# Moving side work to other places inside the turns of the last attention stage

## The chip, the cores and the metric

The kernel runs on one core of one Trainium2 chip. The metric is the device time of one execution in microseconds (us). A profiled execution gives the trace, whose times run from the start of its span.

## What is computed

The reference is a decoder of two layers over 32 sequences of 128 tokens with 256 features, all in float32. Each layer adds three blocks to a running x: layer 0 a state-space block, a cross attention and an attention with a mixture of experts; layer 1 a recurrence, an attention and a mixture of experts. The change lies in the last two blocks, here cut short:

```python
# layer 1, attention: 16 heads of 16 features, over x and over the context, mixed by a gate
q, k, v = split(x @ Wqkv + bqkv);  qa, ka, va = split(ctx @ Wqkv_aux + bqkv_aux)
h_main = softmax(q @ k.T * scale) @ v
h_aux  = softmax(q @ ka.T * scale) @ va
x = x + (h_main * (1 - gate) + h_aux * gate) @ Wo + bo
# layer 1, experts: 2 of 8 per token
xf = layernorm(x)
scores = sigmoid(xf @ gate_w.T + balance_bias)
w, idx = top_k(scores, 2);  w = w / (w.sum(-1) + 1e-6)
x = x + sum over the two chosen experts of w * (silu(xf @ w1[e].T) @ w2[e].T)
```

## The kernel before

The 32 sequences are 8 groups of 4 (512 tokens, `NG = 8`). The attention in question has the tag "e"; its tiles begin with `e_`. It takes one **turn** per group, and a turn has 8 **pairs** of units; a unit is 8 maps of 128x128. For each unit TensorE (PE) makes the scores (line 1390), VectorE (DVE) takes the maximum (1447) and subtracts it (1451), ScalarE (ACT) takes the exponential (1511), GpSimd (POOL) adds halves and quarters of the rows (1544, 1547), PE transposes the maps (1399) and ACT copies them (1507). For each pair DVE finishes the sums and inverts them (1458, 1462, 1465: "invert"), PE turns the inverses (1421), ACT copies them (1517, tile `e_rT`), PE multiplies by the values (1413), and DVE scales and joins the result (1478, 1480: "mix").

Beside these pairs a turn carries **side work** for other groups:

- front: twelve products for the next group, through the one PSUM bank `FB` (two transposes of the normalised x, then q, k, v), each copied away by ACT (lines 1286, 1290, 1297, 1305);
- early: statistics (DVE 1223), scale (POOL 1240 to 1243) and normalisation (ACT 1271) for the group after that;
- back: the two output products of the group before (PE 1574, `FB` too) and the additions into X (DVE 1605, 1607);
- routing of the group before: statistics (DVE 765), scale (POOL 781 to 784), normalised rows (ACT 792), two transposes (PE 806) and copies (ACT 798), the product with the gate weights (PE 812), the addition of the bias (DVE 774), an exponential (ACT 828), the choice of two experts (DVE 836 to 866) with a ranking product (PE 820 to 823), and eight indirect DMAs from POOL that write the rows to their expert's place in DRAM (878, "scatters").

In the last turn there is no next group. Instead the turn holds the first output product of its own group, a total (PE 885) and the **early table**: 21 chained small DVE operations plus the first (926 to 943) that work out for the first 21 places of the expert list where each starts and which expert it belongs to. Each of the chain waits for the one before. `ready_places` is raised between line 908 and line 941.

The order of all this is written by hand. The pairs' program of each engine is a generator that stops at certain places; the side work carries due places, and `weave` (line 34) runs a side step at the first stop whose number is not below its due place:

```python
def weave(main, side):
    due = next(side, None)
    for step in main:
        while due is not None and due <= step:
            due = next(side, None)
```

In pair d (0 to 7) PE stops at 10d (after the next pair's scores, ahead of the transposes of unit 2d+1), 10d+2 (ahead of the values), 10d+5 (ahead of the turning of the inverses and the transposes of unit 2d+2) and 10d+8. DVE stops at 10d+2 (after the softening of unit 2d+2, ahead of invert), 10d+4 (ahead of the softening of unit 2d+3), 10d+6 (ahead of mix) and 10d+8. ACT stops at 10d+2 (ahead of the exponential of unit 2d+2), 10d+4 (ahead of the copy of the inverses and of the maps of unit 2d+2), 10d+6 (ahead of the exponential of unit 2d+3) and 10d+8. POOL stops at 10d (ahead of the sums of unit 2d+2), 10d+4 (ahead of those of unit 2d+3) and 10d+8. So a due place of 17 and one of 18 are the same place on PE; 12 and 13 are not.

All engines run their own queue in order, and a step whose input is not there holds back all behind it. `FB` is one bank: its users follow one another in an order (`fb_order`) that is worked out from the same due places.

After the last turn the stage goes over to the expert list (`list_experts`, lines 2626 to 2780): SyncE (SP) waits for the scatters of group 6 and for `ready_places`, then loads rows and weights place by place (2677, 2680), PE multiplies (2705, 2718), POOL adds the results to the output by indirect DMAs (2778). The routing of the last group (`LAST["route"]`) is woven into this list.

## Time and profile before

| what | value |
|---|---|
| median of 3 runs (lowest, highest) | 3130.05 us (3126.87, 3141.59) |
| the profiled execution's own time | 3133.9 us |
| its span | 3131.8 us |
| busy, share of the span: PE, DVE, ACT, POOL | 86%, 61%, 49%, 48% |
| first and last maximum (line 1447) of this attention | 2214.5, 2821.2 us |
| first load of the expert list | 2832.69 us |
| last scatter of the kernel begins | 3123.1 us |

The attention "e" is thus about 620 of the 3132 us, and the expert list about 290. The three runs lie 14.7 us apart. The spans of the trace are hardware records of each instruction; PE's are modelled at their ends, POOL's are rough.

### The profile page before, as it was taken

How to read it: one execution, taken by the hardware profiler on the slowest of the kernel's cores; microseconds unless marked ns; L12 is line 12 of the kernel's file. 1: busy time of each engine (PE TensorE's matmuls, PEld its weight loads, DVE VectorE, ACT ScalarE, POOL GpSimd, SP SyncE). 2: the span in 40 equal slices, each digit the busy share in tenths (PEclk: the TensorE clock that was granted, in tenths of full speed). 3: DMA queues.
4: the chain of work that ended last, by engine and by line, in shares of the span. 5: the costliest groups of instructions: out<-in, count | busy, mean ns of one | idle time of the engine just before them, and what ended most of it. 6: DMA issues, size and time to landing. Idle time of an engine off the chain costs nothing.

```text
span 3131.8 us, 49455 instructions
## 1 busy us (share of the span) xinstructions
PE 2695.4 (86%) x16576; PEld 1837.2 (59%) x16576; DVE 1900.0 (61%) x3513; ACT 1523.1 (49%) x2641; POOL 1499.7 (48%) x1619
## 2 busy tenths in 40 slices
PE   5888888876988888879999999899888888878997
PEld 2333333323666566645788887697455555557886
DVE  3788888784888788863222222501688988883211
ACT  4566665553777666630122221443666666643322
POOL 3577666673555577625322222200345555553443
PEclk8999999988999999989999999899999999978998
DMA  9700000001005000002377775200000100006875
GB/s 324 245 0 1 0 1 1 1 0 37 15 20 190 1 1 0 1 22 95 117 212 209 209 212 146 71 1 1 1 18 30 37 33 31 22 20 188 228 216 167
DMA packets 137955, 244.73 MB, mean 78 GB/s; under 512 B 15936, under 2 KB 111424, under 8 KB 127040
## 3 DMA queue, kind: packets, MB, share of 16 engines
q1 hardware_dynamic: 111168, 207.61, 20.1%
q0 software_dynamic: 26592, 34.63, 5.6%
q8 instruction: 109, 1.79, 0.2%
q14 instruction: 86, 0.70, 0.1%
HBM read 151.28 MB, written 92.73 MB: 78 GB/s over the span
## 4 chain that ended last, share of the span: by engine, by line
PE 35%; DVE 6%; issue 6%; POOL 5%; ACT 2%; DMA 1%; another core or an unknown queue 0%; POOLq 0%; DVEq 0%; ACTq 0%
PE PS L2442 11%; PE PS L2398 6%; PE PS L2066 4%; PE PS L2705 3%; PE PS L2718 3%; POOL e_hs L1544 2%; DMA out<-e_dead,f_token 1%; DVE e_mx L1447 1%; POOL e_qs L1547 1%; PE PS L1399 1%; POOL rows_in_place L878 1%; PE PS L2057 1%; PE PS L1337 1%; DVE e_pr L1451 1%; DVE e_den L1458 1%
## 5 line engine op out<-in xcount | busy, mean ns | idle before, releaser
L578 POOL TENSOR_TENSOR u_in<-dtx,b_rep 128x512 f32<-128x512 f32 x256 | 325.4, 1294 | 201.3 <-ACT b_rep L559 200.1
L594 DVE TENSOR_TENSOR_SCAN state<-PS,u_in 128x512 f32<-128x512 f32 x256 | 312.3, 1220 | 59.3 <-POOL u_in L578 34.9
L551 PE MATMUL PS<-scaled,ident 128*128 128x512 f32 x512 | 295.6, 661 | 28.7 <-DVE scaled L588 28.7
L2459 ACT ACTIVATE d_act_b<-PS 128x256 f32<-128x256 f32 (+2 forms) x192 | 76.5, 400 | 446.4 <-PE PS L2442 426.4
L1544 POOL TENSOR_TENSOR e_hs<-e_pr 128x512 f32<-128x512 f32 x128 | 163.0, 1273 | 236.5 <-ACT e_pr L1511 232.9
L1544 POOL TENSOR_TENSOR u_hs<-u_pr 128x512 f32<-128x512 f32 x128 | 166.3, 1299 | 215.1 <-ACT u_pr L1511 214.6
L2442 PE MATMUL PS<-d_unit_T,d_w 128*128 128x256 f32 (+1 forms) x1280 | 260.6, 356 | 1.1 <-ACT d_unit_T L2452 1.1
L2362 POOL DMA_INDIRECT out_by_token<-d_y_rows,d_token x71 | 110.8, 1561 | 300.2 <-DVE d_y_rows L2489 201.6
L2468 DVE TENSOR_TENSOR d_hid<-d_act_b,PS 128x256 f32<-128x256 f32 (+2 forms) x192 | 84.4, 441 | 279.9 <-ACT d_act_b L2459 245.6
L567 ACT ACTIVATE PS<-dt,decay_rate 128x508 f32<-128x508 f32 x256 | 173.4, 686 | 138.0 <-DVE state L594 136.2
L2442 PEld LDWEIGHTS PS<-d_unit_T,d_w 128*128 128x128 f32 x1280 | 221.0, 190 | 26.3 <-DVE d_hid L2468 1.3
L588 DVE TENSOR_TENSOR scaled<-state,PS 128x512 f32<-128x512 f32 x256 | 169.4, 664 | 55.9 <-PE PS L532 44.3
L1447 DVE TENSOR_REDUCE u_mx<-PS 128x8 f32<-128x1024 f32 x128 | 155.9, 1218 | 67.9 <-PE PS L1390 67.8
L2398 PE MATMUL PS<-d_w,d_hid 128*128 128x256 f32 x824 | 186.8, 380 | 3.6 <-DVE d_hid L2468 2.6
L2778 POOL DMA_INDIRECT out<-e_dead,f_token x71 | 110.8, 1561 | 158.1 <-DVE f_token L2756 68.2
L1507 ACT ACTIVATE e_pT<-PS 128x1024 f32<-128x1024 f32 x128 | 130.8, 1022 | 103.2 <-PE PS L1399 103.2
L1447 DVE TENSOR_REDUCE e_mx<-PS 128x8 f32<-128x1024 f32 x128 | 155.8, 1217 | 40.6 <-PE PS L1390 40.5
L2398 PEld LDWEIGHTS PS<-d_w,d_hid 128*128 128x128 f32 x824 | 155.6, 190 | 30.2 <-issue 7.5
L1399 PE MATMUL PS<-ident,e_pr 128*128 128x128 f32 x1024 | 148.2, 292 | 25.8 <-ACT e_pr L1511 25.3
L1507 ACT ACTIVATE u_pT<-PS 128x1024 f32<-128x1024 f32 x128 | 131.2, 1025 | 74.2 <-PE PS L1399 73.9
L551 PEld LDWEIGHTS PS<-scaled,ident 128*128 128x128 f32 x512 | 97.2, 204 | 117.9 <-DVE scaled L588 87.1
L1451 DVE TENSOR_TENSOR u_pr<-PS,u_mx 128x1024 f32<-128x1024 f32 x128 | 156.7, 1224 | 9.3 <-POOL u_hs L1544 2.2
(453 smaller groups left out, 6145.2 us busy)
## 6 DMA issues: line engine op xcount, KB each, us to landing
d_w<-in_d_w SPq DMA_DIRECT2D x42, 1024.0 KB, 5.8
e_dead<-in_f_w SPq DMA_DIRECT2D x40, 1024.0 KB
rows_in_place<-blank SPq DMA_DIRECT2D x136, 272.0 KB, 4.1
d_w<-in_d_w SPq DMA_DIRECT2D x42, 512.0 KB
rows_by_expert<-zeros SPq DMA_DIRECT2D x36, 272.0 KB, 3.1
d_unit_rows<-rows_by_expert SPq DMA_DIRECT2D x31, 272.0 KB
e_dead<-rows_in_place SPq DMA_DIRECT2D x31, 272.0 KB
X<-in_x SPq DMA_DIRECT2D x8, 512.0 KB, 11.2
```

The costliest lines, as they stand in the source:

```text
L551: nc.tensor.matmul(YB[:, c], ident[:], scaled[:, (KD * n + c) % RC], start=False, stop=n == NS - 1).then_inc(m_y, 1)
L567: nc.scalar.activation(seqs(DECAY[:, k % RD])[:, :, 1:L], seqs(dt[:, p, c])[:, :, 1:L], ACT.Exp, scale=decay_rate[:, c * NS + n:c * NS + n ...
L578: nc.gpsimd.tensor_tensor(u_in[:, k % RU], dtx[:, p, c], b_rep[:, n % RB], ALU.mult).then_inc(m_u, 1)
L588: nc.vector.tensor_tensor(scaled[:, k % RC], state[:, k % 2], CB, ALU.mult).then_inc(m_hc, 1)
L594: nc.vector.tensor_tensor_scan(state[:, k % 2], DECAY[:, k % RD], u_in[:, k % RU], 0.0, ALU.mult, ALU.add).then_inc(m_h, 1)
L1399: step = nc.tensor.transpose(TR[:, m], pr[:, i % 2, m], ident[:])
L1447: nc.vector.tensor_reduce(mx[:, i % 2], scores_of(i), AX.X, ALU.max).then_inc(maxed, 1)
L1451: nc.vector.tensor_tensor(pr[:, i % 2], scores_of(i), mx[:, i % 2].unsqueeze(2).broadcast_to([128, MAPS, L]), ALU.subtract).then_inc(shift ...
L1507: nc.scalar.activation(pT[:, i % 2].rearrange("p h q -> p (h q)"), flat(PS[:, 4:6]), ACT.Copy).then_inc(taken, 1)
L1544: nc.gpsimd.tensor_tensor(hs[:, i % 2], pr[:, i % 2, :, 0:L // 2], pr[:, i % 2, :, L // 2:L], ALU.add).then_inc(halved, 1)
L2398: step = nc.tensor.matmul(out_h[:, n], hid[:, p, f, row:row + 128], w_down[:, r, f], start=f == 0, stop=f == FC - 1)
L2442: step = nc.tensor.matmul(b, wt[:, r, c, f * 128:f * 128 + 128], x, start=c == 0, stop=c == KD - 1)
```

## The change

Only numbers in the tables of due places are changed (`PLAN["e"]`, `ROUTE`, `LAST`). No operation is added or removed, and the sequence of the users of `FB` stays the same. The routing of the last group, `LAST["route"]`, and the due places of the total stay.

```diff
-        "e": dict(front=[2, 12, 18, 18, 22, 42, 48, 52, 55, 60, 62, 70],
-                  taken=[2, 14, 14, 18, 22, 42, 46, 52, 54, 58, 64, 74], back=[0, 8], out_at=[2, 8],
-                  early=[16, 30, 48]),
+        "e": dict(front=[2, 13, 17, 17, 22, 41, 48, 51, 55, 59, 62, 71],
+                  taken=[1, 14, 15, 17, 23, 44, 45, 51, 53, 58, 63, 76], back=[0, 4], out_at=[2, 8],
+                  early=[16, 23, 47]),
     }
-    ROUTE = dict(stats=14, scale=8, norm=18, turn=[25, 32, 32], taken=[26, 28], add=36, exp=34,
-                 route=[36, 46, 46, 48], rank=50, scatter=[50, 50, 54, 58, 58, 64, 68, 68])
-
-    LAST = dict(back=[52, 0], out_at=[54, 2], total=54, early_table=58, late_total=58, late_table=62,
+    ROUTE = dict(stats=13, scale=8, norm=18, turn=[28, 30, 32], taken=[28, 28], add=34, exp=31,
+                 route=[36, 46, 46, 48], rank=49, scatter=[49, 49, 49, 52, 64, 77, 77, 77])
+
+    LAST = dict(back=[50, 0], out_at=[49, 2], total=54, early_table=71, late_total=58, late_table=62,
```

Put through the stops above, these steps really move (all others fall on the same stop as before):

| step | engine | stop before | stop after |
|---|---|---|---|
| front 1, second transpose | PE | 12 | 15 |
| front 11, last value product | PE | 70 | 72 |
| copy of q, first half (front 2) | ACT | 14 | 16 |
| copy of k (front 4) | ACT | 22 | 24 |
| copy of q, second half (front 5) | ACT | 42 | 44 |
| last copy of values (front 11) | ACT | 74 | 76 |
| second output product of the group before | PE | 8 | 5 |
| scale for the group after next | POOL | 30 | 24 |
| transposes of the routed rows | PE | 25, 32 | 28, 30 |
| first copy of them | ACT | 26 | 28 |
| bias added to the router's sums | DVE | 36 | 34 |
| exponential of them | ACT | 34 | 32 |
| eight scatters | POOL | 50, 50, 54, 58, 58, 64, 68, 68 | 50, 50, 50, 54, 64, 78, 78, 78 |
| last turn: first output product of its group | PE | 52 | 50 |
| last turn: its addition into X | DVE | 54 | 52 |
| last turn: early table, three parts | DVE | 58, 62, 62 | 72, 74, 76 |

## Rows read from the trace of the kernel before

**Rows 1.** Busy time by window, one line a turn; the columns stand on top
```profile
core 0: us, PE busy (x) PEld busy (x) DVE busy (x) ACT busy (x) POOL busy (x), PEclk, DMA share, GB/s
...
2525.66:2600.79 75.13, 64.12 (x579) 42.97 (x579) 67.45 (x130) 49.59 (x72) 43.65 (x49) 0.98 0.09 30
...
2754.66:2831.98 77.32, 51.77 (x443) 37.39 (x442) 61.23 (x128) 33.15 (x41) 36.14 (x38) 0.72 0.06 22
```

**Rows 2.** Waits of DVE, 2525.66 to 2600.79: us in total, times, longest
```profile
DVE e_mx L1447 <- PE PS L1390: 2.6, 5, 0.7
...
DVE e_den L1458 <- POOL e_qs L1547: 1.6, 2, 1.1
...
DVE e_part L1478 <- ACT e_rT L1517: 0.4, 1, 0.4
```

**Rows 3.** Timeline, a turn's start: start, us, engine, line, operation [idle <-releaser]
```profile
2523.89 0.38 ACT L1517 ACTIVATE e_rT<-PS 128x256 f32<-128x256 f32 x1 [0.25 <-PE PS L1421]
...
2524.62 1.89 PE L1574 MATMUL PS<-e_wo,e_oT 128*128 128x256 f32 x8
...
2526.91 1.27 POOL L1544 TENSOR_TENSOR e_hs<-e_pr 128x512 f32<-128x512 f32 x1 [1.11 <-ACT e_pr L1511]
...
2527.28 1.45 DVE L1607 TENSOR_TENSOR X<-X,e_o 128x512 f32<-128x512 f32 x1
...
L1607 DVE TENSOR_TENSOR X<-X,e_o x16: 691/886/1457, 2293.5 to 2840.8; 128x512 f32<-128x512 f32 x16
```

**Rows 4.** Timeline of the same turn, pairs 1 to 3
```profile
2535.51 0.69 ACT L1290 ACTIVATE e_q<-PS,e_bq 128x512 f32<-128x512 f32 x1 [2.82 <-PE PS L1337]
...
2550.70 0.69 DVE L1458 TENSOR_REDUCE e_den<-e_qs 128x16 f32<-128x512 f32 x1 [1.07 <-POOL e_qs L1547]
...
2550.77 1.95 PE L812 MATMUL PS<-f_wr,f_xT 128*128 128x8 f32 x16 [0.69 <-ACT f_xT L798]
...
2550.91 1.07 POOL L1241 TENSOR_TENSOR e_rs<-e_rs,neg_half 128x4 f32<-128x4 f32 x1
...
2551.71 0.36 DVE L1465 COPY e_rec<-e_den 128x128 f32<-128x128 f32 x2
...
2554.38 0.18 DVE L774 TENSOR_TENSOR f_lg<-PS,f_v 128x32 f32<-128x32 f32 x1
```

**Rows 5.** Timeline, its pair 5, then pairs 0 and 5 of the last turn
```profile
2573.49 1.26 POOL L1544 TENSOR_TENSOR e_hs<-e_pr 128x512 f32<-128x512 f32 x1 [0.46 <-issue]
...
2756.87 0.69 DVE L1605 TENSOR_TENSOR e_o<-PS,e_bo 128x512 f32<-128x512 f32 x1 [1.47 <-PE PS L1574]
...
2801.58 2.63 PE L1574 MATMUL PS<-e_wo,e_oT 128*128 128x256 f32 x8
```

**Rows 6.** Timeline of the last turn's end: DVE, PE, POOL and SP's queue
```profile
2809.97 0.16 DVE L926 TENSOR_TENSOR f_count<-PS,f_first_row 128x8 f32<-128x8 f32 x1
...
2814.30 0.16 DVE L934 TENSOR_TENSOR_SCAN f_ends<-f_ones,f_units_e 128x8 f32<-128x8 f32 x1
...
2819.09 0.17 DVE L943 TENSOR_TENSOR f_sent<-f_sent,f_units_e 128x8 f32<-128x8 f32 x1
...
2821.37 0.69 PE L1421 MATMUL PS<-ident,e_rec 128*128 128x128 f32 x2 [6.13 <-DVE e_rec L1465]
...
2827.95 0.69 DVE L1458 TENSOR_REDUCE e_den<-e_qs 128x16 f32<-128x512 f32 x1 [3.58 <-POOL e_qs L1547]
...
2829.36 0.96 POOL L878 DMA_INDIRECT rows_in_place<-f_rows,f_slot  x1 [0.30 <-issue]
...
2831.98 0.42 DVE L1478 TENSOR_TENSOR e_part<-PS,e_rT 128x256 f32<-128x256 f32 x1 [2.66 <-ACT e_rT L1517]
...
2832.69 0.40 SPq L2677 DMA_DIRECT2D e_dead<-rows_in_place  x1
```

**Rows 7.** What SP's queue waited for, 2700 to 2900 us
```profile
SPq L2669 <- DMA rows_in_place<-f_rows,f_slot: 72.7, 1, 72.7
```

**Rows 8.** Busy time by window, the expert list, columns as in group 1
```profile
2900.00:3000.00 100.00, 100.00 (x491) 88.07 (x490) 20.90 (x78) 30.03 (x83) 47.63 (x32) 1.00 0.83 228
```

## The prediction

> **What bounds the kernel now.** I read the busy time by window first. The change touches only the turns of the attention "e", so its turns are the place to look. A turn in the middle takes 75.13 us, and DVE is busy for 67.45 us of it; PE has 64.12, ACT 49.59, POOL 43.65 [rows 1]. DVE bounds these turns. Then the waits of DVE: within that turn it waits 2.6 us for scores (five times), 1.6 us for the sums of POOL (twice) and 0.4 us for the copied inverses, 4.6 us in all [rows 2]; what is left of the 7.7 us are gaps between instructions. So moving side work can't give more than about 4.6 us a turn plus what DVE's own instructions are stretched by. It can cost more, because a step that DVE reaches too early makes it wait with everything behind it.
>
> The last turn is another case: 77.32 us, DVE busy 61.23 [rows 1], so it waits far more, and the timeline shows for what. The early table stands between two softenings and the next invert, from 2814.30 to 2819.26, and PE's turning of the inverses stands idle for 6.13 us behind it. At the end of the turn DVE waits 3.58 us for POOL and 2.66 us for ACT with nothing to do [rows 6]. Then SP's queue loads the first rows of the expert list, at 2832.69; it had waited for a scatter to land [rows 7], whose issue ended at 2830.32 [rows 6], so landing took 2.37 us. In the list PE is busy for 100.00 of 100 us [rows 8]: the list takes its time wherever it starts, and a start that is x us earlier ends the kernel x us earlier.
>
> **The change part by part, in a middle turn.** No instruction is added or removed, so the sum consists of shifts in waits. Steps whose due place changes within the same stop cost nothing.
>
> (a) The second output product (PE 1574, 1.89 us) goes from behind the turning of the inverses and the transposes of unit 2 to ahead of them. What follows on PE's queue comes 1.9 us later: ACT's copy of the inverses, which ended at 2524.27 [rows 3], ends near 2526.1. DVE's mix, with which the turn's window begins, wants it at 2525.66 [rows 1], so it waits 0.4 us. Unit 3's exponential is late by as much, and so POOL's sum from 2526.91 to 2528.18. This takes it off DVE's addition into X: that took 1.45 us from 2527.28, ending 0.55 us after POOL's, while the shortest of its 16 instances took 0.69 [rows 3]. So 0.76 us come back, and half of it goes in the later sums. Between +0.4 and -0.8 us; I take 0, as gain and loss come from the same shift.
>
> (b) ACT's copy of q stood ahead of the inverses and of the maps and let ACT wait 2.82 us for its product [rows 4]. It goes behind them. DVE did not wait there (its waits on the copied inverses are 0.4 us in the turn [rows 2]), so nothing is won at once; the second transpose goes behind the values, the products of q and k come some 0.6 us later, and with them the next scores. 0 to +0.3 us; I take 0.2.
>
> (c) Pairs 2 and 3: the exponential of unit 7 no longer stands behind the copy of the routed rows, which would shorten DVE's wait of 1.07 us for the sums [rows 4]. But POOL's scale chain, 1.07 us for its power [rows 4] and three shorter steps, now stands right ahead of those sums. The transposes go behind PE's own, and the scores of unit 8 come about 0.6 us later, into the same wait. Between -0.9 and +0.6; I take 0.
>
> (d) The bias addition (DVE 774) ran at 2554.38, behind the softening of unit 9. It now stands directly behind the invert, which ends at 2552.07, and needs PE's product, which ends at 2552.72 [rows 4]. DVE waits 0.65 us there, with the softening of unit 9 queued behind it. ACT's exponential of the router also moves, ahead of the exponential of unit 8, and waits for the same addition, so unit 8's exponential, PE's transposes and ACT's copy of them come later too. They have room as long as DVE is the bound. The ends are 0, if the product comes earlier with unit 7's exponential (c), and +1.95, if the product's whole length passes through ACT and PE to the next scores. I take 0.35, near the middle between 0 and the 0.65 that the rows show, for the product should come a little earlier.
>
> (e) Three scatters ahead of the sums of unit 12 instead of two: these came at 2573.49 [rows 5], and one scatter is 0.96 us and a gap of 0.30 [rows 6], 1.3 us. At most +1.0 us on POOL, which waits for ACT elsewhere; on DVE 0 to +0.5, I take 0. The three at the end of the turn stand ahead of the next turn's sums of unit 2, and POOL waits for ACT there too: 0, or in the worst case the same +0.5. The last value product and its copy move by one stop behind work of the pair itself: 0.
>
> Sum per middle turn: 0 + 0.2 + 0 + 0.35 + 0 = about +0.5 us; six turns (those of groups 1 to 6; the first carries no routing) give +3 us. With all ends: -1.7 to +3.8 us a turn.
>
> **In the last turn.** The second output product of group 6 comes earlier, and here DVE waited 1.47 us for it [rows 5]: -1.4 us. It is followed by a stretch with (c) and (d) as above: about +0.1. The group's own first product, 2.63 us on PE at 2801.58 [rows 5], now goes ahead of the transposes of unit 11, which come at least as much later. DVE has that product's addition into X to do meanwhile, which also comes earlier; I count +0.3 us for it in the next step, and at most 2.6.
>
> The early table: its second and third part hold DVE for 4.96 us, and the first, from 2809.97 [rows 6], is mostly beside the scores of the next pair, which DVE would else wait for. All this leaves the place ahead of invert: 5 to 6 us, of which I let 4.8 reach the last invert, as ACT and PE of the pair then bind (with the 0.3 above). The last invert, which ended at 2829.32 (2831.98 less 2.66), would end at 2824.5. The first part fits into DVE's wait of 3.58 us ahead of it. Parts two and three follow: `ready_places` after 4.4 us, at 2828.9; mix at 2829.5 instead of 2831.98. On POOL three scatters instead of two follow the last sums: the last one would begin at 2829.36 - 4.8 + 1.3 = 2825.9 and land at 2829.2. SP goes at the later of 2828.9 and 2829.2: 3.5 us earlier than 2832.69. Together with the 1.3 us from the turn's start: -4.8 us. The ends: -7 (only the table's block counts, and the early product adds all it can) and 0 (the list starts no earlier because the scatters that were put back gate it).
>
> **Sum.** 3133.9 + 3.0 - 4.8 = 3132.1 us against the profiled execution. That lies 3.85 us above the median of the three runs, so the median would be 3128.2; I say 3128.
>
> **A rule against (a) and (c).** The row of the addition into X, 1.45 us beside POOL's sum and 0.69 alone, shows that the two engines hold one another up [rows 3]. The Trainium skill, page "SBUF — State Buffer", section "Summary: rules for kernel authors", says that a DVE instruction with two inputs in SBUF and a GpSimd instruction that reads SBUF block each other for their whole length, and advises to schedule whichever is off the critical path; by it, every side step moved next to such a pair may cost a whole POOL instruction. What would follow from rows alone: one more of DVE's two-input steps a turn that falls under a sum is +0.76 us, seven turns +5 us, so 3133; one fewer gives 3123. It lies within the range.
>
> **The rivals.**
>
> 1. The turns get better, not worse: ACT's waits of 2.82 us and PE's late turning go, and with them most of DVE's wait of 1.07 us and the stretch of 0.76 us. For it: each is in the rows [rows 3, 4]. Against it: the chain of POOL is put just there. At -1.8 us a turn, 6 x -1.8 - 4.8 = -15.6: 3114.5. Chance 0.15.
>
> 2. Slower: DVE and ACT reach the bias addition too early (d). It waits for the product with the gate weights, and the exponential of unit 8 waits behind it on ACT; if PE and ACT can't take that in, each turn pays 1.95 us, and with the other ends of (b) and (e) up to 3.2. Seven turns: +14 to +22, less 4.8 for the end: 3139 to 3147 against the median. It decides from the point where the product ends over 1.5 us behind the invert (0.65 now). For it: the gate product follows two transposes that are themselves moved back. Against it: 1.07 us of waiting right before can absorb it. Chance 0.10, a third of it beyond +0.5%.
>
> 3. The end gives nothing: the scatters moved to the last stop, or the table, gate the list just as late, and turns go as forecast: 3130 + 3 - 1.4 = 3131.6. Against it: both came out at 2829 above, with 3.5 us to spare. Chance 0.15.
>
> The forecast itself has 0.60. A measurement of this kernel can tell about 0.5% (15.7 us) from no change; the three runs alone spread over 14.7 us. Rival 1 passes that bound in a good half of its cases, plus a little from runs that spread: faster 0.13; slower 0.06; within 0.5% 0.81. The range, 3113 to 3142, holds rival 1 at its size, the forecast, rival 3 and the lower end of rival 2.
>
> **What would show it.** (a) In a middle turn the copy of the inverses of pair 0 ends about 1.9 us later against the turn, and the second addition into X takes near 0.7 us. (c) DVE's wait for the sums in pair 3 is below 1.07 us. (d) DVE waits for line 812 ahead of line 774, by 0.65 us or so. The length of a middle turn is then 75.6 us, give or take one. In the last turn no wait of 6 us is left on the turned inverses, the table stands behind the last invert, and from the turn's first mix (2754.66 here) to SP's first load there are 73.2 us instead of 78.0. The list itself keeps its length. I am wrong if middle turns change by over 2 us, or if the distance from that mix to SP's load does not shrink.

## The result, and the profile after

| | kernel before | changed kernel |
|---|---|---|
| median (lowest, highest), 6 runs each | 3130.59 (3126.87, 3141.59) | 3112.86 (3110.43, 3123.00) |
| the profiled execution's own time, span | 3133.9, 3131.8 | 3123.0, 3121.1 |
| ratio, 95% interval | | 0.9942 [0.9929, 0.9956] |

The change saves 17.7 us, 0.6%. The forecast was 3128, so a gain of 2; the time fell just below the range (3113). The sign was right and the size far off.

In the trace I measure the stage from its first mix to SP's first load of the expert list, since what lies outside differs between executions of the same code. Before: from 2228.28 to 2832.69 us, 604.4. After: from 2219.83 to 2805.70 us, 585.9. That is 18.5 us less, of the size of what the medians differ by. Outside, the changed kernel's profiled execution (the slowest of its six) reached the stage 8.4 us earlier and spent 16.3 us more from that load to its end (before: 299.1, after: 315.4). A second profiled execution of it spent 303.4 us there, and those of all experiments 299 to 306, so it does not come with the edit. PE is as full as in [rows 8] from 2900 to 3000 us; in the last 75 us of that execution it waits 9.8 us in all for weights of the experts to land, where the kernel before has 1.9 and the second execution 3.0.

Busy time by window of the changed kernel, one middle turn and then the last turn; columns as in [rows 1]:

```profile
2513.77:2588.43 74.66, 62.60 (x581) 42.06 (x580) 68.14 (x129) 49.84 (x71) 43.16 (x49) 1.00 0.09 30
2739.08:2805.48 66.40, 45.09 (x438) 31.93 (x436) 58.89 (x127) 33.04 (x41) 35.94 (x39) 0.81 0.07 26
```

The last turn (from its first to its last mix) is 10.9 us shorter; with SP's load, which now follows that last mix by 0.22 us instead of 0.71, it is 11.4. The middle turn is only 0.5 us shorter. What is left comes from turns 1 and 6, which no row of mine had looked at:

| us | turn 0 | 1 | 2 | 3 | 4 | 5 | 6 | last, to SP's load | stage |
|---|---|---|---|---|---|---|---|---|---|
| before | 69.54 | 77.19 | 75.53 | 75.12 | 75.13 | 75.60 | 78.27 | 78.03 | 604.4 |
| after | 69.95 | 74.66 | 74.66 | 74.67 | 74.66 | 76.10 | 74.55 | 66.62 | 585.9 |
| difference | +0.41 | -2.53 | -0.87 | -0.45 | -0.47 | +0.50 | -3.72 | -11.41 | -18.5 |

**The turn's start, after** (timeline, answers to [rows 3]; columns: start, us, engine, line, operation):

```profile
2511.05 1.99 PE L1574 MATMUL PS<-e_wo,e_oT 128*128 128x256 f32 x8
...
2513.30 0.38 ACT L1517 ACTIVATE e_rT<-PS 128x256 f32<-128x256 f32 x1 [1.79 <-PE PS L1421]
...
2513.77 0.42 DVE L1478 TENSOR_TENSOR e_part<-PS,e_rT 128x256 f32<-128x256 f32 x1 [0.15 <-ACT e_rT L1517]
...
2515.16 0.69 DVE L1607 TENSOR_TENSOR X<-X,e_o 128x512 f32<-128x512 f32 x1
...
2516.21 1.27 POOL L1544 TENSOR_TENSOR e_hs<-e_pr 128x512 f32<-128x512 f32 x1 [1.96 <-ACT e_pr L1511]
L1607 DVE TENSOR_TENSOR X<-X,e_o x16: 691/693/694, 2285.2 to 2813.0; 128x512 f32<-128x512 f32 x16
```

The copy of the inverses ends 0.09 us ahead of the mix that wants it, where there were 1.39. POOL's half sums begin 2.44 us behind the mix instead of 1.25, and all sixteen additions into X take 0.69 us, none 1.45. This is step (a) as foretold, though the copy comes 1.3 us later against the mix and not 1.9, and the mix waits 0.15 us for it instead of the 0.4 foretold.

**The invert of pair 3, after** (answers to [rows 4]), and behind it two rows of the kernel before that [rows 4] does not have:

```profile
2536.30 1.93 PE L812 MATMUL PS<-f_wr,f_xT 128*128 128x8 f32 x16
...
2537.09 0.69 DVE L1458 TENSOR_REDUCE e_den<-e_qs 128x16 f32<-128x512 f32 x1 [0.41 <-POOL e_qs L1547]
...
2538.38 0.19 DVE L774 TENSOR_TENSOR f_lg<-PS,f_v 128x32 f32<-128x32 f32 x1
...
2538.60 0.23 ACT L828 ACTIVATE f_lg<-f_lg 128x32 f32<-128x32 f32 x1 [1.07 <-DVE f_lg L774]
```

```profile
2553.97 1.92 PE L1399 MATMUL PS<-ident,e_pr 128*128 128x128 f32 x8
...
2554.59 0.23 ACT L828 ACTIVATE f_lg<-f_lg 128x32 f32<-128x32 f32 x1 [2.01 <-DVE f_lg L774]
```

The wait for the sums is 0.41 us instead of 1.07, as (c) said. But DVE does not wait for the gate product, against (d): it ends at 2538.23, ahead of invert (2538.46). ACT waits 1.07 us for the addition; in the kernel before it had waited 2.01.

**The end of the last turn, after** (answers to [rows 6]; then SP's wait, to [rows 7]):

```profile
2796.96 0.16 DVE L926 TENSOR_TENSOR f_count<-PS,f_first_row 128x8 f32<-128x8 f32 x1
...
2799.71 0.69 DVE L1458 TENSOR_REDUCE e_den<-e_qs 128x16 f32<-128x512 f32 x1 [0.85 <-POOL e_qs L1547]
...
2801.00 0.17 DVE L934 TENSOR_TENSOR_SCAN f_ends<-f_ones,f_units_e 128x8 f32<-128x8 f32 x1
...
2802.33 1.01 POOL L878 DMA_INDIRECT rows_in_place<-f_rows,f_slot  x1 [0.30 <-issue]
...
2805.28 0.17 DVE L943 TENSOR_TENSOR f_sent<-f_sent,f_units_e 128x8 f32<-128x8 f32 x1
2805.48 0.42 DVE L1478 TENSOR_TENSOR e_part<-PS,e_rT 128x256 f32<-128x256 f32 x1
2805.70 0.40 SPq L2677 DMA_DIRECT2D e_dead<-rows_in_place  x1
SPq L2669 <- DMA rows_in_place<-f_rows,f_slot: 63.2, 1, 63.2
```

The wait of 6.13 us on the turned inverses is gone. The first part of the table lies in DVE's wait for POOL, of which 0.85 us are left out of 3.58; parts two and three run behind the last invert, while PE and ACT turn and copy its inverses. The last scatter lands 2.36 us after its issue ends (2803.34 to 2805.70), and SP starts by it. The order of these events is the one that the prediction had given.

### The profile page after: what moved, and what is told of

The parts are those of the page before. It is cut to its first block, busy times and chain, and to the rows that moved or that the text cites. A ratio compares the mean times of both kernels' runs of the same rounds, so it can differ in the third digit from the quotient of the medians.

```text
span 3121.1 us, 49454 instructions
## 1 busy us (share of the span) xinstructions
PE 2683.0 (86%) x16576; PEld 1830.6 (59%) x16576; DVE 1899.2 (61%) x3513; ACT 1524.5 (49%) x2641; POOL 1494.5 (48%) x1619
## 4 chain that ended last, share of the span: by engine, by line
PE 33%; POOL 8%; issue 6%; DVE 6%; DMA 2%; ACT 2%; POOLq 0%; SPq 0%; DVEq 0%; ACTq 0%
PE PS L2442 11%; PE PS L2398 6%; PE PS L2066 4%; POOL e_hs L1544 3%; PE PS L2705 3%; PE PS L2718 3%; POOL e_qs L1547 2%; DMA out<-e_dead,f_token 2%; POOL rows_in_place L878 1%; PE PS L2057 1%; DVE e_mx L1447 1%; DVE e_pr L1451 1%; PE PS L2427 0%; PE PS L1337 0%; PE PS L2215 0%
## 5 line engine op out<-in xcount | busy, mean ns | idle before, releaser
L1399 PE MATMUL PS<-ident,e_pr 128*128 128x128 f32 x1024 | 139.4, 280 | 28.6 <-ACT e_pr L1511 28.3
```

The lines of the kernel that those rows point to most:

```text
L1399: step = nc.tensor.transpose(TR[:, m], pr[:, i % 2, m], ident[:])
```

## The experiments

Turns below are read as in the table above: from first mix to first mix. The window of pair d runs from the mix of pair d to the next mix, so it holds the invert of pair d+1. Stage, turns and pairs of a run come from its one profiled execution. Two of the changed kernel gave 585.9 and 586.0 us; single turns with the same instructions differ by up to 2 us between executions, as experiments 2 and 3 show.

**1. The table alone.** `early_table=58` becomes 71.

> Only the early table goes to due place 71; all else is the kernel before. Theory 1 (what the profile after shows: the whole table block of 6.9 us was on DVE's path, and nothing of it comes back behind the last invert): from the last turn's first mix to SP's first load there are 78.0 - 7 = 71 us, SP's load is set by the scatter that lands last, and the whole kernel is 7 us faster (ratio 0.9978). Theory 2 (my prediction: the scores and the late transposes cover part of it): 4.8 us or less, 73.2 to 74.5 us. Middle turns keep 75.1 us under both.

Ratio 0.9986 [0.9968, 1.0004]. The last turn to SP's load takes 72.14 us instead of 78.03; its pair 5 falls from 14.31 to 7.47 and its pair 6 grows from 8.36 to 10.87. Stage 598.5. One us of these 5.9 lies in the first five pairs, above all in pair 0 (11.72 to 10.75), ahead of all that moved. From the sixth mix to SP's load it is 23.4 against 18.5 us. So the table by itself gives some 4.9 us, not the 3.5 of my sum nor the 7 of theory 1.

**2. The whole line of the last turn** (`LAST` as changed, and the router's `rank=49`, which keeps the order of `FB`).

> The table and the last group's own first product with its addition move (the whole LAST line of the change; the rank product's due place goes from 50 to 49, which is the same stop). Theory 1: the product adds at most 0.5 us to what the table alone gives, so 71 to 71.5 us from first mix to SP's load. Theory 2 (the product ahead of the transposes keeps PE busy and its clock at full level, and helps): about 69 us.

Ratio 0.9984 [0.9972, 0.9997]; last turn 72.31, stage 599.0. The group's earlier output product adds nothing to the table. Turns 5 and 6, where nothing was moved, are worth a look: 77.20 and 76.60 us, where the kernel before has 75.60 and 78.27. The one with the granted clock at 0.86 in pair 0 is turn 5 here and turn 6 there. So with the same instructions such a fall costs 1.6 us, in either turn.

**3. The routing alone** (`ROUTE` as changed, all else as before).

> Only the ROUTE line moves. My prediction: a middle turn gets 0.35 to 0.6 us longer (75.5 to 75.7), since DVE waits ahead of the bias addition. Rival: the turn gets shorter, since the copies of the routed rows no longer stand ahead of the attention's own: 74.5 or less. In the last turn the three scatters behind the last sums make SP's load 1.3 us later than before by the prediction, unless pairs 2 to 4 give back as much: 78 to 79 us against 75 to 76 by the rival.

Ratio 0.9977 [0.9962, 0.9992], stage 598.0, turns 76.65, 74.22, 74.23, 76.97, 75.34, 75.34, last turn 75.66. Two turns are as the rival said (74.5 or less), the others fit neither. The last turn is 2.4 us shorter: its first four pairs give 4.5 (pair 3 falls from 12.99 to 11.49, pair 0 from 11.72 to 9.92), the rest of the turn takes 2.1 back.

What separates turn 2 (74.22) from turn 2 of experiment 6 (74.98), which has the same instructions and the full clock too, is pair 0: 11.84 us against 12.60. The addition into X and POOL's half sums begin within 0.04 us of each other here, and which of them is long depends on which comes second. Turn 2, then turn 4:

```profile
2376.23 0.69 DVE L1607 TENSOR_TENSOR X<-X,e_o 128x512 f32<-128x512 f32 x1
2376.24 1.81 POOL L1544 TENSOR_TENSOR e_hs<-e_pr 128x512 f32<-128x512 f32 x1 [0.99 <-ACT e_pr L1511]
...
2524.64 1.27 POOL L1544 TENSOR_TENSOR e_hs<-e_pr 128x512 f32<-128x512 f32 x1 [0.94 <-ACT e_pr L1511]
2524.68 1.77 DVE L1607 TENSOR_TENSOR X<-X,e_o 128x512 f32<-128x512 f32 x1
```

**4. The plan alone** (`PLAN["e"]` as changed, all else as before).

> Only the PLAN line of e moves. My prediction: a middle turn stays within 0.2 us of 75.13, and the last turn is 1.4 us shorter (76.6 us from first mix to SP's load), as DVE no longer waits 1.47 us for the second output product. Rival: the q copy that no longer blocks ACT, and the product ahead, give the whole gain of a middle turn, 74.7 us or less.

Slower: ratio 1.0040 [1.0019, 1.0061], stage 614.2, turns 76.70, 78.25, 78.41, 78.41, 78.40, 79.24. A third of the change, taken alone, costs 9.8 us of stage, although the last turn is 3.2 us shorter (74.87); both theories are missed. The windows of pairs 0, 1 and 2 of turn 3 (columns as in [rows 1]; the third number from the end is the granted clock) say what is odd:

```profile
2452.90:2464.69 11.79, 8.91 (x71) 5.95 (x70) 11.37 (x30) 6.91 (x9) 5.59 (x8) 0.86 0.14 46
2464.69:2474.46 9.77, 7.98 (x69) 4.41 (x68) 6.70 (x13) 7.57 (x12) 4.55 (x6) 1.00 0.00 0
2474.46:2485.59 11.13, 8.97 (x86) 7.15 (x87) 8.59 (x19) 5.70 (x9) 5.03 (x7) 0.85 0.01 2
```

TensorE's granted clock falls in pair 0 and again in pair 2, in each of turns 2 to 5, and the pair that follows the first fall is 9.77 us where the kernel before has 7.55.

**5. Does the clock do it? The plan alone, and a little work that nobody reads.** Four transposes of the identity go into the free bank `FB`, in every turn but the last, 28 in all, after the same wait as the next product:

```diff
+                if table and j == 1 and g > 0:
+                    yield 12
+                    after(pe, empty, product("front", g, j))
+                    for k in range(GS):
+                        nc.tensor.transpose(FB[:, k * L:k * L + L], ident[:], ident[:])
                 yield at[j]
```

> The old kernel with the new PLAN line (turns of 78.4 us, with the granted clock at 0.86 in pair 0 of turns 2 to 5) and, ahead of the values of pair 1, four more PE transposes (0.66 us) of the identity into FB, in time that PE waits for ACT's copy. They compute nothing that is used. Theory of the clock: they fill the stretch after which the clock falls, it stays at 1.00 in pair 0, pair 1 takes 7.3 to 8.2 us instead of 9.77, and the turn is 1.5 to 2.4 us shorter with more work. Rival (order alone makes the turn long): 78.4 us or more.

3129.8 us in one execution, stage 602.9 instead of 614.2, turns 76.72, 75.69, 76.33, 76.72, 75.70, 77.21. Pairs 0, 1 and 2 of turn 2:

```profile
2368.03:2379.82 11.79, 9.35 (x78) 5.38 (x76) 11.37 (x30) 7.62 (x9) 5.75 (x9) 1.00 0.13 44
2379.82:2387.97 8.15, 6.37 (x66) 4.03 (x66) 7.20 (x13) 6.97 (x11) 4.36 (x6) 1.00 0.01 2
2387.97:2399.10 11.13, 8.22 (x90) 5.77 (x88) 8.60 (x19) 7.12 (x10) 5.02 (x7) 1.00 0.00 0
```

PE does more and the stage is 11.3 us shorter. Pair 0 has the full clock in all turns, and pair 1 falls from 9.77 to 8.15. Turn 1 of experiment 4, which kept the clock in pair 0 without help, has 8.15 there as well. The clock still falls in pair 2 of turns 1, 3, 4 and 6. In pair 3 of just these turns, and of turns 1 to 6 of experiment 4, the copy of the inverses (line 1465) takes 1.44 us beside POOL's half sums, which then begin some 0.02 us behind it; in turns 2 and 5 it takes 0.36. That is a second way in which a fall costs time: it shifts POOL's sums onto the copy (more on this in experiments 10 and 11). Hence most of the loss in experiment 4 is the clock; the shifts of the plan cost only some 0.2 us in a turn without a fall (75.69 against 75.53).

**6. Routing and last line, the plan as before.**

> The changed kernel with the old PLAN line: only ROUTE and LAST are new. If the parts add up, the first mix to SP's first load takes 604.4 - 6.5 (routing alone) - 5.5 (last line alone) = 592.4 us, against 585.9 of the changed kernel, and PLAN is worth 6.5 us here though it costs 9.8 us alone. Middle turns of 74.2 us where the clock stays, 76.6 to 77 where it falls.

Ratio 0.9940 [0.9918, 0.9963], stage 590.2: turns 76.47, 74.98, 74.98, 74.97, 74.96, 74.96, last turn 69.29. The plan on top of these gives 4.3 us more, where alone it cost 9.8. Its worth hangs on what else is there.

**7. The changed kernel once more.**

> The changed kernel as it is, beside the next two on the same chip. Its structure should come back: middle turns of 74.7 us, 66.6 us from the last turn's first mix to SP's first load, a ratio of 0.994. The theory on the clock (a fall costs a turn 1.3 to 2.4 us and hits few turns of this kernel) expects one or two turns of 76 us, at the same or at another place.

Ratio 0.9937 [0.9916, 0.9958], stage 586.0, last turn 67.08. One turn of six is longer than 74.7 here too, but it is turn 4 (75.82, its pair 4 10.22 us at a clock of 0.83) and not turn 5.

**8. Step (a) alone.** On the kernel before, `back=[0, 8]` becomes `[0, 4]`.

> Kernel before with one edit: the second output product of the previous group goes ahead of the turning of the inverses (due place 4 instead of 8). The prediction's step (a): between -0.8 and +0.4 us a turn, 0 taken. From the changed kernel, where the same step stands: the addition into X falls from about 1.45 to 0.7 us and pair 0 of a middle turn shortens from 12.60 to about 11.8 us. Theory A (the shift alone does this): pair 0 is 11.8 to 12.0, a middle turn without a fall of the clock 74.3 to 74.8 (before 75.1 to 75.6). Rival B (the shorter pair 0 needs the other moves of the plan): pair 0 stays within 0.3 of 12.60. Either way, if the granted clock falls in pair 0 of a turn, pair 1 is 1.3 us or more longer there. One look only, so the time itself is told to within some 10 us: 3118 to 3135.

3123.2 us in one execution, stage 597.1, turns 75.21, 75.26, 75.25, 75.24, 75.65, 75.78, last turn 74.88. Pair 0 of a middle turn is 11.79 us instead of 12.60, as theory A has it, and pair 7 9.07 instead of 8.83: -0.57 us together. Yet the turns are not the 74.3 to 74.8 us of that theory. In turns 1 to 5 the clock is 0.84 in pair 2, and pair 3 is 11.1 us, so that turns 2 to 5 add up to what they were before. The 7.3 us of stage lie in turn 1 (2.0), turn 6 (2.5) and the last turn (3.2). A part of this is the clock, which no longer falls in pair 0: in turn 1 it fell there in all five kernels without step (a) (the one before, experiments 1, 2, 3 and 6) and in none of the kernels with it. Turn 6 shows what that does. Before: the windows of its pairs 0 and 1, then PE's product of q, ACT's copy of it and the next mix:

```profile
2676.39:2688.99 12.60, 9.49 (x71) 5.94 (x71) 10.44 (x21) 4.80 (x8) 6.06 (x9) 0.86 0.13 44
2688.99:2697.86 8.87, 7.95 (x67) 4.18 (x66) 6.65 (x11) 8.68 (x13) 2.50 (x3) 1.00 0.00 0
2685.00 2.89 PE L1337 MATMUL PS<-e_dead 128*128 128x512 f32 x4
2687.93 0.69 ACT L1290 ACTIVATE e_q<-PS,e_bq 128x512 f32<-128x512 f32 x1 [4.50 <-PE PS L1337]
2688.99 0.42 DVE L1478 TENSOR_TENSOR e_part<-PS,e_rT 128x256 f32<-128x256 f32 x1 [1.78 <-ACT e_rT L1517]
```

The same three with step (a) alone:

```profile
2675.11 1.88 PE L1337 MATMUL PS<-e_dead 128*128 128x512 f32 x4
2677.03 0.69 ACT L1290 ACTIVATE e_q<-PS,e_bq 128x512 f32<-128x512 f32 x1 [3.00 <-PE PS L1337]
2678.10 0.42 DVE L1478 TENSOR_TENSOR e_part<-PS,e_rT 128x256 f32<-128x256 f32 x1
```

The product takes 2.89 us at the low clock and 1.88 at the full one. ACT's copy of q stands ahead of its copy of the inverses, and so DVE's mix waits 1.78 us, or not at all.

**9. Step (d) undone.** The changed kernel with `add=36, exp=34`.

> Changed kernel with step (d) undone: the bias addition and the router's exponential back to due places 36 and 34. The prediction's (d) said that the early place costs 0.35 us a turn (0 to 1.95). Theory of (d): undone, a middle turn shrinks from 74.66 to about 74.3. Rival (the product already stands when the invert ends, so the early place is free, and the exponential of unit 8 gains from it): a middle turn stays at 74.66 or grows by up to 0.5 us, and the pair from the third to the fourth mix stays within 0.3 of 10.08. First mix to SP's first list load: 583 to 590 us.

3116.3 us in one execution. A turn without a fall of the clock is 75.07 us instead of 74.66: pair 2 10.35 against 10.08, pair 3 10.57 against 10.43. So the early place of the bias addition is worth 0.4 us in such a turn, as the rival said. The stage does not show it, 585.9 us in both: turn 5 of the changed kernel lost 1.4 us with a fall in pair 0, which did not come here. The rows:

```profile
2543.94 1.93 PE L812 MATMUL PS<-f_wr,f_xT 128*128 128x8 f32 x16
...
2548.41 0.18 DVE L774 TENSOR_TENSOR f_lg<-PS,f_v 128x32 f32<-128x32 f32 x1
2548.63 0.23 ACT L828 ACTIVATE f_lg<-f_lg 128x32 f32<-128x32 f32 x1 [2.51 <-DVE f_lg L774]
2548.89 0.18 DVE L836 TENSOR_SCALAR f_lg<-f_lg 128x32 f32<-128x32 f32 x1 [0.29 <-ACT f_lg L828]
```

The late addition lets ACT wait 2.51 us with the copies of the inverses and of the maps behind it, and the next unit's exponential behind those; DVE waits 0.29 us for the router's.

**10 and 11. A collision inside the change.** After the change pair 6 of each turn is 9.30 us instead of 8.22. The inverse's copy is stretched beside POOL's half sums, which begin 0.03 us behind it:

```profile
2575.62 1.44 DVE L1465 COPY e_rec<-e_den 128x128 f32<-128x128 f32 x2
2575.65 1.32 POOL L1544 TENSOR_TENSOR e_hs<-e_pr 128x512 f32<-128x512 f32 x1 [1.07 <-ACT e_pr L1511]
```

The row joins two copies. In the trace's single instructions the first takes 0.23 us in every turn and the second, which begins 0.14 us later, 1.30 us, in each of turns 0 to 6; elsewhere it takes 0.22.

The scatters alone do not bring this about. Experiments 3 and 6 have no scatter at 68 either, and their pair 6 is 8.22. Experiment 6 there:

```profile
2585.52 0.36 DVE L1465 COPY e_rec<-e_den 128x128 f32<-128x128 f32 x2
...
2586.28 1.27 POOL L1544 TENSOR_TENSOR e_hs<-e_pr 128x512 f32<-128x512 f32 x1 [1.80 <-ACT e_pr L1511]
```

With the old plan POOL waits 0.73 us longer for the exponential. PE's transposes stand behind the last value product there (1344; they begin 2.4 us ahead of the copy) and ahead of it in the changed kernel (3.2 us ahead of the copy). In experiment 4, new plan and old scatters, the pair is 8.23, but in turn 0, which carries no scatters, it is 9.08 there against 7.99 before. So the collision needs both: the last value product one stop later (front 11) lets the exponential come earlier, and no scatter holds POOL's sums back.

I put one scatter back ahead of these sums (`scatter=[..., 68, 77, 77]`, `early_table=70`), then two (`[..., 68, 68, 77]`, with `early_table` at 71 again).

> The changed kernel with one scatter due at 68 instead of 77, and the early table due at 70 instead of 71. Theory of the port: in pair 7 of each turn of the changed kernel the copy of the inverses (DVE 1465) takes 1.44 us instead of 0.36, since POOL's sum 1544 starts 0.03 us after it; a scatter ahead of that sum starts it some 0.3 to 1.3 us later, the copy takes 0.36 again, and every turn is 1.07 us shorter: 73.6 us in the middle, 7.5 us in all. Rival (the copy is long for another reason, or the later sum is then waited for by the next invert): 74.7 us as before. The table one stop earlier and two scatters instead of three behind the last sums: SP's load 1 to 1.7 us earlier in the last turn, 65 us from its first mix.

> Changed kernel with two of the three late scatters at due place 68 instead of 77, so that they run ahead of the sums in the pair that follows. In the changed kernel the copy of the inverted sums takes 1.44 us there instead of 0.36, beside POOL's half sums that begin within 0.1 us of it, and the pair is 9.30 us instead of 8.22. Theory (the collision decides): POOL's half sums begin 1.0 to 1.3 us later, the copy falls back to 0.36, the pair to 8.2 to 8.4, and a middle turn to 73.6 to 73.9 us: six turns, -5 to -6.5 us, ratio to the kernel before 0.992 against 0.994 of the changed kernel. Rival (two more POOL steps ahead of the sums make DVE wait for them instead): the pair stays at 9.2 or grows to 9.6, DVE shows a wait for the sums there of 0.5 us or more, and the ratio is 0.994 or above.

With one scatter the pair stays long (9.35 us, stage 585.9, ratio 0.9950 [0.9932, 0.9968]): the half sums begin 0.12 us behind the first copy and are still in time for the second, which takes 1.35 us. The last turn is 65.6 us, near the 65 expected, and turns 5 and 6 take that back. Two scatters did move it:

```profile
2576.96 0.36 DVE L1465 COPY e_rec<-e_den 128x128 f32<-128x128 f32 x2
2577.36 0.96 POOL L878 DMA_INDIRECT rows_in_place<-f_rows,f_slot  x1 [0.30 <-issue]
2578.34 1.28 POOL L1544 TENSOR_TENSOR e_hs<-e_pr 128x512 f32<-128x512 f32 x1
```

The pair is 8.22 us and turn 1 takes 73.59, 1.07 less, as the theory said. Yet the stage is 585.8 us and the ratio 0.9938 [0.9917, 0.9958]: no gain. Turns 2 to 6 are 74.77, 75.06, 75.03, 75.10 and 75.85. The windows of pairs 0 and 1 of turn 3:

```profile
2438.60:2450.39 11.79, 8.91 (x71) 5.75 (x70) 11.36 (x29) 7.05 (x9) 5.59 (x8) 0.86 0.14 46
2450.39:2459.15 8.76, 8.17 (x70) 4.51 (x68) 6.62 (x12) 7.63 (x13) 3.79 (x4) 1.00 0.00 0
```

The clock falls in pair 0 of turns 3 to 6 and takes back 1.5 us a turn; in turn 2 it falls in pair 4 (10.23 us instead of 8.88). In turn 6 the collision also comes back one invert later, in pair 7: a second copy of 1.31 us, the pair 9.92 us against 9.06. The kernel before has the same in its turn 6 (1.30 and 9.91).

**12. The same with the four transposes of experiment 5.** (The first turn has them too, other than the expectation says.)

> The version with two scatters at 68, and in every turn but the first and the last TensorE does four transposes of the identity into the free bank at its stop 12, whose results nobody reads. With two scatters at 68 alone the late pair of each turn fell from 9.30 to 8.22 us as meant, but in turns 3 to 6 the granted clock fell to 0.83 to 0.86 in pair 0, and the pair that follows took 8.76 to 10.65 us instead of 7.28 (9.16 in turn 6), so that first mix to SP's first list load stayed at 585.8. Theory (the gain of the mended pair was eaten by the clock, and a little added work in pair 0 keeps it): the clock is 1.00 in pair 0 of all turns, turns 1 to 5 take 73.6 to 74.0 us, first mix to SP's load is 578 to 582, the ratio to the kernel before 0.990 to 0.993. Rival (the clock falls in another pair instead, or four transposes delay the values as much as they save): at least three of the turns stay at 74.8 or above and the distance at 584 or above, ratio 0.993 to 0.995.

Stage 579.8 us, turns 73.59, 73.61, 73.59, 73.59, 73.60, 74.37. The same windows:

```profile
2458.70:2470.49 11.79, 9.34 (x78) 5.38 (x76) 11.36 (x30) 7.63 (x9) 5.74 (x9) 1.00 0.14 46
2470.49:2477.78 7.29, 6.69 (x67) 4.13 (x66) 7.12 (x13) 7.17 (x12) 3.54 (x4) 1.00 0.00 0
```

In the trace the theory holds, turns and stage as expected: no fall in any of the six turns, 5.9 us of stage. The whole time does not show it: ratio 0.9938 [0.9920, 0.9957], against 0.990 to 0.993 expected. The profiled execution reached its first mix at 2241.53 us, that of experiment 11 at 2220.30, with the same code ahead. What makes that part vary was not looked into.

**13. Twelve such transposes a turn** (also ahead of the products due at 22 and 51).

> The same with four identity transposes ahead of two more of the front's products (due 22 and 51), 12 a turn in all. Theory (what is left of clock falls lies in pairs 2 and 4, where one turn of the version with two scatters at 68 took 10.23 us at 0.83 instead of 8.88): no granted clock below 0.97 in any pair of turns 1 to 6, and a distance from first mix to SP's load that is 0 to 2 us below the run with one group of four. Rival (added work delays transposes and scores more than it saves): the distance is 1 to 4 us longer than with one group.

Stage 579.7 us. Two turns had a fall after all, other than the theory said: turn 4 (75.16, its pair 4 10.61 at 0.84) and turn 1 (pair 2 at 0.85), and turn 1 is the shortest of all (72.93). Median 3113.2 against 3136.8 of the kernel before on that chip (their quotient is 0.9925), ratio 0.9913 [0.9895, 0.9931]. The stage is that of experiment 12, so the two ratios differ by what lies outside it. That it is ahead of the changed kernel (0.9942 and 0.9937) is not shown: the intervals overlap.

**14. Added work in the last turn,** seven times eight transposes, with two scatters at 68.

> The same as the run with two scatters at 68, and in the last turn TensorE also does seven times eight transposes of the identity into the free bank at seven of its stops: work that nobody reads. Without them the granted clock of that turn is 0.56, 0.70, 0.82 and 0.57 in its pairs 1, 3, 4 and 6, and TensorE idles some 20 of 66 us. Theory (the low clock of the last turn costs time, because DVE waits for scores and ACT for transposes): the granted clock of the turn rises to 0.9 or above in these pairs, and from the turn's first mix to SP's first load there are 2 to 4 us less. Rival (DVE and POOL bind there, the clock is free, and the added work only stands in the way): clock up or not, the distance stays the same or grows by up to 2 us.

Ratio 0.9944 [0.9923, 0.9964]; the last turn to SP's load is 67.13 us, against 66.43. Its pairs 3 and 6, first without the added work (experiment 11), then with it:

```profile
2768.18:2779.66 11.48, 8.44 (x68) 5.87 (x68) 10.86 (x24) 4.43 (x5) 5.70 (x6) 0.70 0.01 1
2796.68:2805.85 9.17, 4.49 (x42) 3.20 (x42) 7.38 (x29) 2.57 (x4) 5.68 (x6) 0.57 0.17 62
```

```profile
2772.22:2783.99 11.77, 6.77 (x76) 5.12 (x76) 11.15 (x24) 4.54 (x5) 5.99 (x6) 1.00 0.00 0
2801.20:2810.61 9.41, 2.61 (x42) 1.87 (x42) 7.61 (x30) 2.80 (x4) 5.74 (x6) 0.91 0.17 60
```

The clock rose from 0.70 to 1.00 and from 0.57 to 0.91 (it stayed at 0.56 and 0.82 in pairs 1 and 4), and the pairs grew by 0.29 and 0.24 us. DVE's busy time grew by as much, 0.29 and 0.23, so its idle time stayed at 0.6 and 1.8 us at either clock. There the low clock had been free.

## Why the prediction was wrong, step by step

| step | predicted | measured |
|---|---|---|
| turn 0 | 0 | +0.4 |
| turns 2 to 5 | +2.0 | -1.3 |
| turns 1 and 6 | +1.0 | -6.2 |
| last turn | -4.8 | -11.4 |
| stage | -1.8 | -18.5 |

**The step that failed first: one turn stood for six.** I read the turn at 2525.66 and multiplied. Turns 1 and 6 were 2.1 and 3.1 us longer, with the granted clock at 0.86 in their pair 0. Six us of the gain lie there. Experiments 5 and 12 show that such a fall costs 1.5 us or so behind pair 0 and that keeping PE at work avoids it, experiment 2 that with the same instructions it costs 1.6 us; experiment 8 shows that with (a) alone it is gone in turns 1 and 6. Turn 6 also had a copy of 1.30 us in its pair 7 (9.91 us, now 9.06).

The turn that I read was not even a plain one. Turns 3 to 5 of the kernel before have the clock at 0.87 in pair 2, and turns 3 and 4 are 0.4 us shorter for it (75.1 against 75.5 in turn 2): DVE's line 1480, which takes 1.2 to 1.3 us beside POOL's sums in pairs 3 and 4 of turn 2 and 0.29 when clear, is clear there. Against turn 2, the only middle turn with the full clock, the changed kernel gains 0.87 us:

| us, turn 2 | pair 0 | 1 | 2 | 3 | 4 and 5 | 6 | 7 |
|---|---|---|---|---|---|---|---|
| before | 12.61 | 7.54 | 11.00 | 10.62 | 16.71 | 8.23 | 8.82 |
| after | 11.79 | 7.28 | 10.07 | 10.44 | 16.72 | 9.30 | 9.07 |

**(a) The sign was open, and the gain was real.** The mechanism was told right, down to 0.69 us for the addition; the shift was 1.3 us and not 1.9. I set gain against loss and took 0. Measured alone it is -0.81 us in pair 0 and +0.24 in pair 7. The term was mis-sized by 0.6 us a turn, and its effect on the clock was missing, for better (turns 1 and 6) and for worse (pair 2 of turns 1 to 5 in experiment 8, which ate the 0.6).

**(b) "DVE did not wait there, so nothing is won"** holds for a turn at the full clock only. In turn 6 of the kernel before DVE waited 1.78 us behind just this copy. The move of the copy was not tried alone. The whole plan carries it and still lost more in pair 1 when its clock fell (9.77). In the changed kernel pair 1 is 0.26 us shorter. What the move is worth stays open.

**(c) Right in sign of the wait, mis-sized in the sum:** the wait for the sums shrank from 1.07 to 0.41 us, and I had taken 0. Pairs 2 and 3 are 1.1 us shorter together; without (d), 0.7 of that are left for (c) and what the plan moves beside it.

**(d) Wrong in sign.** I took +0.35 us; experiment 9 gives -0.4. I let the product's end stay where the trace of before had it, 0.65 us behind invert. But invert was itself late by the wait of 1.07 us, and PE's product moved with the transposes ahead of it; only their difference counts. And I priced what the step makes wait, but not what it lets go: the copies of the inverses and the maps and the next unit's exponential, which stood behind the router's exponential on ACT while it waited. In the stage of experiment 9 the 0.4 us a turn are covered by a fall of the clock in one turn of the changed kernel.

**(e) "At most +0.5" for the scatters, and 0 for the last value product,** missed what the two do together. Each move alone leaves pair 6 of turns 1 to 6 at 8.2; both together put POOL's sums on DVE's copy, and the pair costs 1.07 us more (experiments 3, 4, 6, 10 and 11). That loss is in the changed kernel, in each of turns 0 to 6, and the other gains cover it.

**The last turn.** The place of every step was right, the size was not. I let 4.8 of the table's 5 to 6 us reach the last invert and then added back that parts two and three stand ahead of the last mix. From the sixth mix to the last invert it was 7.7 us (20.0 to 12.3). The table alone gives 6.1 of them (experiment 1: 13.9) and brings SP's load 4.9 us earlier, where I had 3.5. The block before also included the first part, 1.9 us of DVE at 2809.97, which I had called covered by DVE's wait for scores. PE's own clock, low behind the 6.13 us of idling, is not the cause in pair 5: experiment 1 has 7.47 us there at a clock of 0.57, the changed kernel 7.53 at 1.00. What brings the other 1.6 us was not separated. The start of the turn gave 5.2 us in its first four pairs instead of 1.3. There (a) alone gives 3.2 (experiment 8) and the routing alone 4.5 (experiment 3), so they overlap; I had put the routing's part at +0.1. How much of this is the clock (pair 0 at 0.79 before, 1.00 after) stays open.

**The rivals.** Rival 1 came nearest in time (3114.5), with turns that get better by 1.8 us each; by its own mechanism they gave 0.5 to 0.9. That its time is near the measured one is luck: the rest came from turns 1 and 6 and from the last turn. Rival 2 is ruled out by experiment 9 (the early addition does not lengthen a turn), rival 3 by the last turn. Of my two conditions for being wrong, the distance shrank (66.62; I had said 73.2), but turns 1 and 6 changed by more than 2 us.

**What was not settled:** whether a given pair will lose the clock. The changed kernel itself lost it in turn 5 once and in turn 4 the other time. Nor is a turn settled by its clock alone: experiments 6 and 3 have the same instructions up to the last turn and differ in their turns (74.98 four times against 74.22, 74.23, 76.97, 75.34), in part at the full clock, by which of two engines comes first. And the changed kernel is not free of such collisions: line 1480, 0.29 us when clear, takes 1.04 and 1.30 us in pairs 3 and 4 of its turn 2. No run tried to mend these.

## What to carry to other kernels

Before multiplying one turn's sum by the number of turns, list length and granted clock of every turn, pair by pair; one that differs has a mechanism of its own, and it may hold the larger part of the gain. An edit that mends a collision or a wait can be paid back elsewhere, so judge it by the stage and not by the pair; a few products that nobody reads are a cheap test of whether the clock took the gain. A step that seems to have nothing to do with a collision may be what holds two engines apart: look at what runs beside each step before moving it.

## What the runs showed of the hardware

- The granted clock of a stretch may fall to a mean of 0.83 to 0.87 in a pair of 10 to 13 us in the middle of a stage whose PE is busy for 84% of its time. What PE does then runs at 1.2 GHz and not at 2.4: eight transposes took 1.92 us instead of 1.04 to 1.09, the product of q 2.89 instead of 1.88. Four transposes, 0.6 us of work, went with a clock of 1.00 in all six turns (experiment 12); in experiment 5 pair 2 still lost it in four turns, and in experiment 13 two turns did. The Trainium skill, page "TensorE: Matmul & The Clock Gate", section "What's actually happening", says that the gated clock is the default and activity releases it; the trace agrees. It agrees in that added work went with fewer falls; which pair falls, it does not tell here.
- A low clock costs where someone waits for PE: 1.5 us behind pair 0, nothing in pairs 3 and 6 of the last turn (experiment 14). It can also shift POOL's sums onto a DVE instruction (1.07 us lost, experiments 4 and 5) or off one (0.4 us gained, turns 3 and 4 of the kernel before).
- Of the addition into X and POOL's half sums the second to begin is the long one, whichever engine it is: 0.69 and 1.81 us with DVE 0.01 us ahead, 1.27 and 1.77 us with POOL 0.04 us ahead (experiment 3).
- DVE's copy, which has one input in SBUF, was held up by POOL too: two copies took 0.36 us in all when clear, and 1.44 beside half sums of 1.32 us that began 0.03 us later. The Trainium skill, page "SBUF — State Buffer", section "Summary: rules for kernel authors", lists a DVE instruction in a two-port mode beside the one with two SBUF inputs, and says that the second to issue is blocked until the first ends. The trace agrees: it is the second of the two copies that is long, 1.30 us instead of 0.22, and it begins 0.11 us behind POOL's sums.
